# Two sets of attention rows instead of three, a seventh slot for the scan's replicated inputs, and another written order of the work

## What is computed

```python
x = x + mamba(norm(x))       # conv, silu, dt = softplus(..), scan over 512 tokens of
                             # h = exp(dt*A)*h + dt*B*xc for 512 channels x 16 states, y = sum(h*C)
x = x + ffn(norm(x))         # silu(x@wg) * (x@wu) @ wd, 768 hidden
x = x + rwkv(norm(x))        # K, V, R; e = exp(clip(W+K)); cumsum(e*V), cumsum(e);
                             # eu = exp(clip(U+K)); WKV = (shift(cumsum eV)+eu*V)/(shift(cumsum e)+eu)
                             # out = (sigmoid(R)*WKV) @ Wo
x = x + ffn(norm(x))
```

## Time and profile before

| | |
|---|---|
| median of 3 runs | 2376.15 us (2371.28 to 2376.19) |
| the profiled execution's own time | 2375.18 us |
| its span in the profile | 2373.4 us |
| mean granted TensorE clock | 0.812 of full speed |
| DVE busy | 1864.1 us (79%) |
| PE busy | 1597.9 us (67%) |
| POOL busy | 1249.9 us (53%) |
| ACT busy | 920.8 us (39%) |

### The profile page before, as it was taken

One profiled execution on the slowest core, in us unless ns is written; L12 is line 12 of the kernel. 1 busy time (PEld: TensorE's weight loads), 2 busy tenths in 40 slices (PEclk: granted clock), 3 DMA queues, 4 the chain that ended last, 5 costly groups with the idle time before them and its releaser, 6 DMA issues. The chain is left out here.

```text
span 2373.4 us, 21200 instructions
## 1 busy us (share of the span) xinstructions
PE 1597.9 (67%) x4800; PEld 768.9 (32%) x4800; DVE 1864.1 (79%) x2430; ACT 920.8 (39%) x1470; POOL 1249.9 (53%) x939
## 2 busy tenths in 40 slices
PE   4352496578855797586955798566965777586757
PEld 1110242333422342243413353233423343243424
DVE  3187897897879898887979988888978968985462
ACT  2343345243633346233543336333452425232321
POOL 0547538752596437843496426854387434741150
PEclk9575698788977898787967899777977888887878
DMA  4322422113311413113311313204221122110100
GB/s 141 145 86 89 134 75 80 54 60 111 104 63 34 151 41 109 49 35 136 101 58 44 122 58 105 71 27 140 79 75 53 51 98 82 45 36 25 38 9 9
DMA packets 124953, 179.33 MB, mean 76 GB/s; under 512 B 10481, under 2 KB 74482, under 8 KB 124850
## 3 DMA queue, kind: packets, MB, share of 16 engines
q1 hardware_dynamic: 124850, 178.36, 22.6%
HBM read 140.05 MB, written 38.27 MB: 75 GB/s over the span
## 5 line engine op out<-in xcount | busy, mean ns | idle before, releaser
L534 POOL TENSOR_TENSOR bu<-rep,bc 128x512 f32<-128x512 f32 x512 | 673.4, 1344 | 571.7 <-PE ps_y L968 535.2
L778 DVE TENSOR_TENSOR_SCAN ps_d<-ps_d,bu 128x512 f32<-128x512 f32 x512 | 625.2, 1221 | 79.9 <-ACT ps_d L645 54.6
L645 ACT ACTIVATE ps_d<-rep,scale_a 128x512 f32<-128x512 f32 x512 | 348.5, 688 | 530.9 <-DVE bu L785 517.4
L907 PE MATMUL ps_r<-mix,wkv 128*128 128x512 f32 x512 | 274.2, 684 | 160.4 <-DVE kv L850 158.1
L968 PE MATMUL ps_y<-bu,sel 128*32 128x512 f32 x1024 | 177.9, 775 | 281.2 <-DVE bu L785 281.1
L785 DVE TENSOR_TENSOR bu<-ps_d,bc 128x512 f32<-128x512 f32 x512 | 344.7, 675 | 0.0
L907 PEld LDWEIGHTS ps_r<-mix,wkv 128*128 128x128 f32 x512 | 107.0, 220 | 322.1 <-issue 320.3
L907 PE MATMUL ps_r<-xT,wgate 128*128 128x512 f32 x384 | 198.7, 642 | 11.8 <-ACT xT L648 11.8
L546 POOL TENSOR_TENSOR kv<-sums,kv 128x1024 f32<-128x1024 f32 x64 | 150.2, 2347 | 106.1 <-DVE sums L864 106.1
L907 PE MATMUL ps_r<-xT,wup 128*128 128x512 f32 x384 | 183.9, 601 | 0.0
L916 PE MATMUL ps_r<-wo,yr 128*128 128x256 f32 x512 | 159.4, 475 | 31.1 <-DVE yr L876 31.1
(11 more groups left out here) (93 smaller groups left out, 2280.0 us busy)
## 6 DMA issues: line engine op xcount, KB each, us to landing
rep<-dd_scratch SPq DMA_DIRECT2D x128, 512.0 KB, 4.3
dd_scratch<-xs SPq DMA_DIRECT2D x32, 512.0 KB, 3.1
bc<-bc_scratch SPq DMA_DIRECT2D x64, 256.0 KB, 4.9
xc_scratch<-xc SPq DMA_DIRECT2D x32, 256.0 KB, 2.0
sz_scratch<-xin SPq DMA_DIRECT2D x32, 256.0 KB, 2.1
xg<-xc_scratch SPq DMA_DIRECT2D x32, 256.0 KB, 2.7
szg<-sz_scratch SPq DMA_DIRECT2D x32, 256.0 KB, 2.9
wr<-w_r_dram SPq DMA_DIRECT2D x64, 128.0 KB, 3.2
```

The source lines that it names most:

```text
L534: pool.tensor_tensor(bu[:, i % BU, :], rep[:, g % REP, 1, :], bc[:, 0, q, :], ALU.mult)\
L645: act.activation(ps_d[D_BANK[i]][:, :], rep[:, g % REP, 0, :], ACT.Exp, scale=scale_a[:, a, NQ * j + q:NQ * j + q + 1]).then_inc(decay_rea ...
L778: dve.tensor_tensor_scan(d[:, :], d[:, :], bu[:, i % BU, :], 0.0, ALU.mult, ALU.add)\
L907: last = pe.matmul(dst, lhs, rhs, start=n == 0, stop=n == len(pairs) - 1)
```

## The change

Two constants, and the written orders:

```diff
-DB, BU, REP, RB, WS, EU = 3, 8, 6, 3, 3, 3
+DB, BU, REP, RB, WS, EU = 3, 8, 7, 3, 3, 2
```

The orders of all five queues are written anew. The stretches of the full round that the prediction speaks of ("..." marks what is left out):

```diff
 PE, first feed-forward
-p_gate.0 p_up.0 p_gate.1 p_up.1 p_in.2 p_gate.2 p_up.2 p_gate.3 p_in.3 p_up.3 p_gate.4 p_up.4 p_gate.5 p_up.5 p_in.4 p_y.0 p_down.0
+p_gate.0 p_up.0 p_gate.1 p_in.2 p_in.3 p_up.1 p_gate.2 p_up.2 p_gate.3 p_up.3 p_gate.4 p_in.4 p_up.4 p_gate.5 p_up.5 p_in.5 p_down.0
 PE, attention b
-p_xproj.0 p_recept.0 p_recept.1 p_recept.2 p_recept.3 p_recept.4 p_dt.0 p_y.3 ... p_k.5 p_wo.0 p_y.5 p_wo2.0 p_wo.1 p_wo2.1 p_v.5
+p_xproj.0 p_dt.0 p_recept.0 p_recept.1 p_recept.2 p_dt.1 p_recept.3 p_recept.4 p_y.3 ... p_k.5 p_wo.0 p_wo2.0 p_wo.1 p_wo2.1 p_v.5
 ACT
-a_xproj.0 a_recept.0 a_decay.15 a_recept.1 a_recept.2 a_decay.16 a_recept.3 a_decay.17 a_recept.4 a_dt.0 a_recept.5 a_decay.18
-a_recept.6 a_recept.7 a_decay.19 a_decay.20 a_eu.0 a_e.0 a_table.0 a_ln.0 a_eu.1 a_e.1 a_dt.1 a_eu.2 a_e.2 a_decay.21 a_ln.1
+a_decay.15 a_xproj.0 a_dt.0 a_recept.0 a_recept.1 a_recept.2 a_decay.16 a_decay.17 a_recept.3 a_decay.18 a_recept.4 a_decay.19
+a_recept.5 a_decay.20 a_recept.6 a_recept.7 a_decay.21 a_decay.22 a_eu.0 a_e.0 a_table.0 a_ln.0 a_dt.1 a_decay.23 a_decay.24 a_eu.1
+a_e.1 a_decay.25 a_ln.1 a_e.2 a_decay.26 a_decay.27 a_rec.0 a_dt.2 a_eu.2 a_e.3 a_ln.2 a_rec.1 a_dt.3 a_eu.3 a_e.4 a_ln.3 a_rec.2
 DVE, round start and first feed-forward
-hv_shift.0 v_scan.0 v_post.0 hv_shift.1 ... v_scan.2 rv_shift.1 v_hc.1 v_conv.0 v_gate_in.0 v_conv.1 v_up.0 v_gate_in.1 v_xc.0 v_up.1
-v_conv.2 v_gate_in.2 v_xc.1 v_up.2 v_gate_in.3 v_scan.3 v_conv.3 v_up.3 v_gate_in.4 v_xc.2 v_up.4 v_hc.2
+hv_shift.0 hv_shift.1 v_post.0 ... v_scan.1 v_hc.0 rv_shift.1 v_conv.0 v_scan.2 v_conv.1 v_gate_in.0 v_gate_in.1 v_up.0 v_xc.0 v_up.1
+v_conv.2 v_gate_in.2 v_xc.1 v_up.2 v_conv.3 v_gate_in.3 v_xc.2 v_up.3 v_gate_in.4 v_sz.0 v_xc.3 v_up.4 v_hc.1 v_scan.3 v_hc.2
 DVE, attention b
-v_scan.18 v_hc.17 v_kd.0 v_scan.19 v_hc.18 v_scan.20 v_kd.1 v_ev.0 v_esum.0 v_evsum.0 v_hc.19 v_kd.2 v_scan.21 v_hc.20 v_scan.22
-v_ev.1 v_wkv.0 v_esum.1 v_evsum.1 v_ev.2 v_kd.3 v_hc.21 v_scan.23 v_hc.22 v_esum.2 v_evsum.2 v_kd.4 v_wkv.1 v_ev.3 v_wkv.2 v_esum.3
-v_evsum.3 v_ev.4 v_kd.5 v_esum.4 v_evsum.4 v_wkv.3 v_scan.24 v_hc.23 v_esum.5 v_scan.25 ... v_esum.7 v_wkv.6 v_evsum.7 ... v_hc.32 v_wkv.7
+v_scan.18 v_hc.17 v_scan.19 v_hc.18 v_scan.20 v_hc.19 v_kd.0 v_scan.21 v_hc.20 v_scan.22 v_hc.21 v_ev.0 v_esum.0 v_evsum.0 v_kd.1
+v_scan.23 v_hc.22 v_scan.24 v_hc.23 v_scan.25 v_kd.2 v_hc.24 v_ev.1 v_esum.1 v_wkv.0 v_evsum.1 v_kd.3 v_ev.2 v_esum.2 v_wkv.1
+v_evsum.2 v_kd.4 v_ev.3 v_esum.3 v_wkv.2 v_evsum.3 v_kd.5 v_ev.4 v_esum.4 v_wkv.3 v_evsum.4 v_scan.26 ... v_esum.7 v_evsum.7 v_wkv.6 ... v_wkv.7 v_hc.32
 POOL, attention b
-g_bu.23 g_clip.0 g_dt.0 g_add.0 g_clip.1 g_num.0 g_clip.2 g_dt.1 g_add.1 g_dt.2 g_num.1 g_add.2 g_clip.3 g_num.2 g_clip.4 g_dt.3
-g_add.3 g_clip.5 g_num.3 g_bu.24 g_add.4 g_bu.25 g_num.4 g_bu.26
+g_bu.23 g_clip.0 g_bu.24 g_bu.25 g_dt.0 g_add.0 g_clip.1 g_num.0 g_dt.1 g_add.1 g_clip.2 g_num.1 g_dt.2 g_add.2 g_clip.3 g_num.2
+g_dt.3 g_add.3 g_clip.4 g_num.3 g_bu.26 g_bu.27 g_bu.28 g_bu.29 g_add.4 g_clip.5 g_num.4
 SP
-s_rep.5 s_gate.0 ... s_wr.4 s_rep.9 s_wr.5 ... s_dt.3 s_rep.10 s_rep.11
+s_rep.5 s_rep.6 s_gate.0 ... s_rep.9 s_rep.10 s_xdbl.0 s_wr.3 s_wr.4 s_wr.5 ... s_dt.3 s_rep.11
```

## The result

The changed kernel took 2403.9 us (median of 4 runs, 2403.45 to 2405.24), the kernel before 2373.72 beside it: a ratio of 1.013, 95% interval 1.0112 to 1.0149. That is 30 us slower. The forecast was 2385, 9 us slower; the sign was right and the size was a third of what came.

A forecast was written before the change was run, and what follows sets the result against it. DVE was busiest at 79%, no engine full, so only idle or hindered time could move. Six full rounds at +1.05 gave +6.3 us, other rounds -1.5, +4 and +0.6: +9.4 on 2375.2, forecast 2385 us, range 2377 to 2394.

The forecast's parts named there:

- seventh slot: Loads of replicated inputs: nobody waits for them, so 0; a whole delay at most 3.4 us a round.
- clock: PE's lone p_k in attention stay near 1.2 GHz; +0.5 us a round for the chance that one link is late.
- scan and rest: Round of scan and rest: DVE stands for POOL's g_add and g_clip in attention, less waits saved; +4 us.
- head and scan: Round of head and scan: two scans move ahead of four g_dt, but the block starts later; -1.5 us.
- last round: Unit cycles grow, +2.8 us to v_wkv.3; v_evsum.7 takes 2.2 of the 3.75 us before v_wkv.7; +0.6 us.
- First feed-forward: Start of a full round: v_up.4 comes one projection later on PE; DVE 1.2 us behind, bounds 0 to +3.1.
- before attention: DVE's 5.5 us of waits for ACT and PE gone but for 0.5, spent on earlier scans, not attention.
- POOL's stretch: Attention, g_dt.0 to end of g_num.3: 49.2 us instead of 51.3, but starting later; v_wkv.3 ends 3.0 us later.
- rival A: Faster: in POOL's attention stretch instructions hinder each other less, each g_dt falling toward 5.4 us; 2363 us, chance 0.30.
- The end of attention: p_y.5 gone from between p_wo.0 and p_wo2.0, -1.5 us; v_hc.32 and v_evsum.7 moved, -0.95 us a full round.
- Rival B: Much slower: two sets make a_ln.2 and a_ln.3 hold g_dt in attention, +4 us a round; 2409 us, chance 0.15.
- Rival C: Nothing: 5.5 us freed before attention and POOL's later start cancel, the slot does nothing; 2376 us within 4, chance 0.13.

The follow-up runs named there:

- experiment 6: Extra unread matmuls in four places a round: first, changed kernel, 2385.74 us; second, kernel before, 2366.63; third, changed orders with six slots and SyncE's old order, 2379.92.
- experiment 9: Four loads moved behind s_gate.0 plus extra matmuls: kernel before, 2354.94 us; changed orders with six slots and two sets, 2365.55; the same with three sets, 2361.29.
- experiment 1: Changed kernel with six slots instead of seven and SyncE's order of the kernel before: 2398.7 us, ratio 1.0111.
- experiment 8: Changed orders of PE, ACT, DVE and POOL, six slots, SyncE's old order with four loads moved behind s_gate.0: 2379.56 us, ratio 1.0019.
- experiment 4: Changed kernel, seven slots, with five loads on SyncE moved behind s_gate.0: 2401.26 us, ratio 1.0129.
- experiment 7: Kernel before with four loads on SyncE (bc.2, bc.3, rep.4, rep.5) moved behind s_gate.0: 2351.53 us, ratio 0.9913.
- experiment 3: Six slots, half of the order changed: old up to v_scan.14, then changed, 2445.19 us; the reverse with three sets, 2380.37; the first mended, 2409.6.

## Why the prediction was wrong, point by point

| Term | forecast | measured | what the runs say |
|---|---|---|---|
| seventh slot | 0 | +5.8 | experiment 6, third to first |
| clock | +0.5 a round for `p_k` | +12 in all | experiment 6; at `p_wo`, not at `p_k` |
| a full round's own order | +0.55 (1.05 less the clock's 0.5) | +0.05 | experiment 6, third against second |
| scan and rest | +4 | +3.7 (+7.4 in the raw pair) | experiment 6, profiles |
| head and scan | -1.5 | +0.3 (+1.3 in the raw pair) | experiment 6, profiles |
| last round | +0.6 | +8.7 (+3.8 in the raw pair) | experiment 6; two sets 5 of it, experiment 9 |

The raw pair are the changed kernel and the one before as they stand. The measured column sums to 5.8 + 12 + 13.3 = 31, for 30 us; the 13.3 are 0.3 for six full rounds, 3.7, 0.3, 8.7 and 0.3 in the start. That the order's own 13.3 lie near the forecast's 9.4 is luck: the 6.3 forecast for six full rounds were 0.3, and the 0.6 for the last round were 8.7.

*Seventh slot.* The step that failed is "they still come before the new round's `g_bu.0` ... Taken as 0". I asked who waits for the loaded data, and nobody does: no wait for rep, as forecast. The delay itself was computed rightly: `s_rep.0` goes out 8.2 us ahead of the end of `v_gate.3` instead of 11.7. I did not ask what else the DMA engines have to carry then. My upper bound, 3.4 us a round, would have held it (the 5.8 are at most 1 us a round).

*First feed-forward, before attention.* `v_up.1` waits 1.56 instead of 2.5, for PE, and `v_scan.14` starts 1.9 us later without the slot's effect (experiment 1, 76.7 against 74.8): the +1.2 was +1.9, inside the bound of 3.1. The 5.5 us of waits for ACT and PE fell to 0.45 and 0.40, as said, and were spent on scans: right.

*POOL's stretch.* 48.7 for 49.2, no hole, `v_wkv.3` at 149.2 (experiment 1) for 149.6, waits of 3.67, 3.33 and 4.30 for "3 to 4". Right; rival A's condition (under 46) was not met.

*Low clock.* I priced it at the `p_k` of attention, and not at `p_wo.0`, though its matmuls took 3.78 us in the trace of before too (at 969.82). The step that failed is "The rest of the round is the same work in nearly the same order, DVE-bound: 0", which let the clock out. In truth PE is on the path from `v_wkv.3` to `v_wo.0`, and whether the clock rises ahead of `p_wo2.0` or after it is 2.7 us. The changed order, which has no `p_y.5` there, fell in the bad case in two of six rounds, in four with six slots (experiment 1), in three in experiment 8 and in all six in experiment 4; in the kernel before `v_wo.0` does not wait for PE at all. So the two long rounds (5.4 us) are luck of the phase, and a forecast could only have had them in its range; what moves the phase from round to round stays open.

*The end of attention.* `p_y.5` away and `v_hc.32` moved: -2.45 forecast; from `v_wkv.3` (+2.6) to the end of a short round (+1.4) experiment 1 gained 1.2, half of it. With the clock out it came whole: in the second to sixth full round of experiment 6, third against second kernel, `v_wkv.3` is 3.5 us later (forecast 3.0), `v_wkv.7` 1.0, and the end of the round 0.

*Outer rounds.* Scan and rest was walked rightly: +4 forecast, +3.7 with the clock out. The other 3.7 of the raw pair are the clock: with the extra matmuls that round falls from 256.5 to 252.5 in the changed kernel and stays at 249.1 in the one before. Head and scan did not get shorter. The last round was under-priced: `v_wkv.3`, forecast +2.8, started 8.6 us later (116.6 against 108.0 in the round). I had added one `g_add` per unit and left out that `v_kd.(i+1)` then waits for PE, 3.61 us each. In the raw pair the rest of that round gave 5 us back: the kernel before loses 5.5 us to the clock there (205.6 against 200.1 with the extra matmuls), the changed one 0.6.

Rival B came nearest in the sum (2409) with the wrong cause: no `a_ln` ended a wait of POOL between `g_dt.0` and `g_num.3`, and three sets changed nothing in full rounds. Rival C is out. One slip of the prediction changes nothing: by its own terms the chances of the same time and of a slower one are 0.18 and 0.52, not 0.19 and 0.51.

## What to carry to other kernels

A buffer more lets loads go out at other times, and the question is not only who waits for them but what they collide with: here the loads of 512 KB at a loop's start cost 3 to 4 us a round under either order, and moving four of them behind a later unit was worth 21.5 us, two thirds of what the whole change lost. Read the waits that have no releaser ("issue") at a loop's first instructions beside the DMA share of that stretch. And before an order of work is judged by a per cent, look whether rounds of equal work have equal lengths: where they don't, the clock's phase is in the number. Compare rounds by cuts at the same unit: two orders can begin a round with different ones, and here that had put 5.8 us into the wrong round.

## What the runs showed of the hardware

In the changed kernel and the one before, the first instruction of a loop's round on DVE waited 4.0 to 5.0 us, without a semaphore, with the DMA engines loaded (busy share 1.03 and 0.67 in the 9 us shown), and 2.3 to 2.6 in experiment 7 (0.23). A second such wait, some 3 us later, was 0.21, 0.99 or 2.68 us by how long the loads lasted. The DMA view of the changed kernel counts packets of the queue of kind "instruction" in that stretch (822.5 to 836):

```profile
q1 hardware_dynamic: 1764, 4.51, 94.0%
q14 instruction: 4, 0.03, 0.7%
```

PE was at 1.2 GHz again when `p_wo.0` came 6.16 us behind the extra matmuls, and at 2.4 when they had ended 0.30 us ahead of it (matmuls of 3.78 and 2.00 us). Extra matmuls helped only where they ended right ahead of the real ones.

What stays open: why `v_conv.0` waits about 1.4 us less for ACT with late loads (seen in two orders, not taken apart), and the 1.5 us by which the changed first half lengthens a full round, which experiment 3 did not split between ACT's and PE's order. Nor did a run take apart the 3.7 us of the round without a head, or the 3.5 of the last round that three sets leave.
